# A two-layer transformer forward on one core: context transfers issued in the FFN with its norm, the output projection inside the int8 attention, casts moved between engines, root tables loaded early

## The chip, the cores and the metric

The kernel is one program for one core of a Trainium2 chip. Its engines run side by side and meet at semaphores: TensorE (PE in the profile; PEld is its weight load), VectorE (DVE), ScalarE (ACT), GpSimd (POOL), and SyncE (SP), which here only issues transfers to the core's 16 DMA engines. The metric is device time in microseconds of one execution. Lower is better.

## The reference, cut to what matters

```python
x = x + _L0_xattn_ref(_layernorm(x), ctx_2048, ...)   # fp8 self and cross attention
x = x + _L0_attn_ref(_layernorm(x), W_Q, W_K, W_V, W_O)          # causal, 16 heads
x = x + _L0_ffn_ref(_layernorm(x), gate_w, up_w, down_w)         # block-scaled fp8 FFN
x = x + _L1_xattn_ref(_layernorm(x), ctx_2048, Wq, bq, Wkv, bkv, Wp, bp)
x = x + _L1_attn_ref(_layernorm(x), wq, wk, wv, wo)              # decaying linear attention
x = x + _L1_ffn_ref(_layernorm(x), gate_w, w_gate_up, ...)       # 32 experts

# _L1_xattn_ref: 16 heads of 32, int8 rounding of q, k, v, 8 bits for the weights
q, k, v = _fq_sym(q, -1), _fq_sym(k, -1), _fq_sym(v, 2)
attn = softmax(einsum('bhqd,bhkd->bhqk', q, k)); attn = _fq_unsigned(attn, -1)
out = einsum('bhqk,bhkd->bhqd', attn, v).transpose(...).reshape(B, N, C)
return out @ Wp + bp
```

`x` is 256 tokens by 512 and the context 4096 by 512, both float32. `_layernorm` divides by the square root of the variance plus 1e-5.

## The kernel before, in words

The residual `x_res` stays in SBUF as two tiles of 128 tokens (`NT` = 2) by 512. The program is a row of stages (`Stage`). Each has its own memory and semaphores, and ends with the semaphores cleared and a barrier over all engines. So no engine starts a stage before the last one has left the stage ahead, SP included; an engine has left when its instructions are done, and for SP that means that they are issued, not that the data has landed.

`layernorm_stage` (L109) is used ahead of three stages: "ln1" ahead of the causal attention, "ln2" ahead of the FFN, "ln4" ahead of the decay attention. GpSimd writes 1e-5 to `eps`. VectorE takes mean and variance of both tiles (`s_var`). ScalarE waits for `eps` and then for each variance and takes the root (L150); a table load for the root stands right ahead of the first one, behind its wait. VectorE inverts and scales (L139, L140), TensorE transposes, and ScalarE and VectorE each copy a half of `xT`. Meanwhile SP issues the transfers that `loads` names.

- ln1's loads: the weights of head pair 0 of the causal attention (`wqkv[0]`), three units of FFN weights, `wo[0]`, and those of pair 1 (`wqkv[1]`, `wo[1]`).
- ln2's loads (`context_loads`, L1180): the context for the int8 attention in four transfers of 2 MB, and four small ones, of which the last is `vbias`, 128 rows of 4 bytes. The transposed `xT2` that ln2 makes is not read; the FFN reads `xn`.
- ln4's loads: `wkv`, `wq`, `rope`, `decay`, `wo` of group 0, then the same four of group 1.

`ffn_stage` (L1043) quantises and restores each normed tile in blocks (`mx_dequantise`, nine VectorE instructions), transposes it, and runs eight steps of gate, up and down products. Its weights are in SBUF by then. It has no work for SP or GpSimd.

`int8_cross_attention_stage` (L1236) goes over `CC` = 4 chunks of `HC` = 4 heads. `int8_order` writes one order of steps, and each engine walks it and does its part. A "slot" is 512 context positions of one tile of queries (u = 2·head + tile): a "first" product whose peak VectorE takes (L1753), and, two u later, a "second" product whose exponential ScalarE takes (L1633). Every second slot has a "turn": TensorE transposes the 8-bit weights of a head (L1510) into one of two PSUM banks `b`, ScalarE (L1640) or VectorE (L1774) casts them to `probT`, and "weigh" multiplies them with the values (L1523). A head has eight turns, j = 0 to 7. `cast_on_vector` says which engine casts: VectorE the even j, in all chunks but the last with one exception in the chunk's last head. In the last chunk there are no key and value products left to make for a next one, and in its last two heads no "first" products either. At the end of a chunk "finish" folds the sums (L1536, L1541) and VectorE writes `outT` (L1779 to L1781).

`projection_stage` (L1814, named "xout") follows as a stage of its own: it loads `w` (1 MB) and `bias`, multiplies `outT` by `w`, and adds both to the residual. Then comes ln4.

The lines that the prediction speaks of:

```python
for kc in range(KC):                                                   # L1181
    sp.dma_start(ctxT[:, kc, :], A["ctxT"][:, kc, :]).then_inc(s_ctx, 16)
...
def cast_on_vector(h, j):                                              # L1298
    return j % 2 == 0 and not (j % 4 == 2 and h % HC == HC - 1 and h // HC + 1 < CC)
...
self.nc.clear_and_free_semaphores(self.sems)                           # Stage.__exit__
self.nc.all_engine_barrier()
```

Of the kernel before, what the change touches and what calls it, by code (L numbers as in the profile page):

```python
# [108 lines left out]
def layernorm_stage(nc, name, C, x, xT, xn=None, loads=None):  # L109

    with Stage(nc, name) as st:
# [4 lines left out]
        std = st.sb("std", [P, NT])  # L116
# [3 lines left out]
        with nc.Block() as block:  # L120
# [641 lines left out]
def causal_attention_stage(nc, C, xT, A, x, ffn_weights, early, loads):  # L762
# [8 lines left out]
    with Stage(nc, "causal") as st:  # L771
# [30 lines left out]
        with nc.Block() as block:  # L802

            @block.sync
            def _(sp):
# [9 lines left out]

                for p in range(NP):
# [226 lines left out]
def ffn_stage(nc, C, xn, weights, x):  # L1043
# [3 lines left out]
    with Stage(nc, "ffn") as st:  # L1047
        deq = [st.sb(f"deq{e}", [P, DM]) for e in range(2)]
# [11 lines left out]
        names = "dequantised turned copied gate_up exp used down dve"  # L1060
        s_q, s_t, s_c, s_g, s_e, s_u, s_dn, s_dve = (st.sem(n) for n in names.split())
        steps = [(f, t) for f in range(NF) for t in range(NT)]
        with nc.Block() as block:

            @block.vector
            def _(dve):
                link = Chain(dve, s_dve).after
                for t in range(NT):
                    mx_dequantise(dve, link, xn[:, t, :], stat, power[:, :], shifted[:, :], deq[t][:, :]).then_inc(s_q, 1)
# [17 lines left out]
            def _(act):  # L1087
                for t in range(NT):
# [57 lines left out]
def build_middle(nc, C, A, x, early):  # L1146
    with ExitStack() as right:
        with ExitStack() as memory:
            weights = memory.enter_context(nc.sbuf_tensor("ffn_weights", [P, FFN_UNITS, 4, P], F32))
            with ExitStack() as inner:  # L1150
# [10 lines left out]
                def loads(sp):  # L1161
# [5 lines left out]
                    sp.dma_start(wqkv[1][:, :, :, :], A["wqkv0"][1]).then_inc(s_w[1], 16)  # L1167
                    sp.dma_start(wo[1][:, :, :], A["wo0"][1]).then_inc(s_wo[1], 16)
# [19 lines left out]
            xn = memory.enter_context(nc.sbuf_tensor("xn2", [P, NT, DM], F32))  # L1188
            xT = memory.enter_context(nc.sbuf_tensor("xT2", [P, KC, TOK], F32))
            layernorm_stage(nc, "ln2", C, x, xT, xn=xn, loads=context_loads)  # L1190
            ffn_stage(nc, C, xn, weights, x)
# [44 lines left out]
def int8_cross_attention_stage(nc, C, A, residual, ctxT, s_ctx, weights, outT):  # L1236
# [8 lines left out]
    with Stage(nc, "int8") as st:  # L1245
# [29 lines left out]
        std = st.sb("std", [P, NT])  # L1275
# [22 lines left out]
        def cast_on_vector(h, j):  # L1298
            return j % 2 == 0 and not (j % 4 == 2 and h % HC == HC - 1 and h // HC + 1 < CC)
# [12 lines left out]
        for step in order:  # L1312
# [7 lines left out]
            if what in ("turn", "key turned", "value turned", "query turned"):  # L1320
# [6 lines left out]
                 "eps var std normed x_turned xT_act xT_dve q_done q_kept q_rounded q_parts")  # L1327
        (s_a, s_aa, s_ad, s_b, s_ba, s_bd, s_vq, s_kf, s_kp, s_pk, s_sc,
         s_out, s_put, s_dve, s_hi, s_rest, s_mid, s_vm, s_vc, s_sum, s_sumc, s_fold, s_kd, s_kk,
         s_eps, s_var, s_std, s_norm, s_xt, s_xa, s_xd, s_qm, s_qk, s_qr, s_qp) = (st.sem(n) for n in names.split())  # L1330

        s_wq = st.sem("wq_loaded")
# [4 lines left out]
        with nc.Block() as block:  # L1337

            @block.sync
            def _(sp):  # L1340
# [12 lines left out]
                for c in range(1, CC):  # L1353
                    load_keys(c)
                    load_values(c)

# [27 lines left out]
            def _(pe):  # L1384
# [158 lines left out]

                pe.wait_ge(s_ctx, 16 * KC)
# [1512 lines left out]
```

## Time and profile before

| | |
|---|---|
| time, median of three runs | 2641.4 us (2641.16 to 2645.72) |
| the profiled execution: its own time, its span | 2642.37 us, 2640.6 us |
| TensorE busy, share of the span | 88% |
| VectorE busy, share of the span | 68% |
| ScalarE busy, share of the span | 47% |
| mean granted TensorE clock | 0.948 of 2.4 GHz |

The span is the time between the first and the last recorded instruction. A timeline row has the start in us from the start of the span, the duration in us, the engine, the line, the instruction, what it writes and reads, and in brackets how long the engine had been idle and what ended that. SPq is SP issuing a transfer; its duration is that of the issue. A PE row for a float32 product counts two instructions for each `matmul` of the code. A window row has the stretch, its length, the busy time of each engine, the mean granted clock as a share of full speed, the share of time that the DMA engines were busy, and GB/s.

### The profile page before, as it was taken

The numbers are of one execution on the slowest core, as the hardware profiler recorded it, in microseconds if no ns is written. First come the engines' busy times: TensorE is split into PE (matmuls) and PEld (weight loads), VectorE is DVE, ScalarE is ACT, GpSimd is POOL, SyncE is SP. The second block draws the span as 40 slices with busy tenths as digits, with TensorE's granted clock in tenths as the row PEclk, the third lists the DMA queues.
The fourth block names the chain that finished last, engine by engine and source line by source line (L and its number), as shares of the span: only waits on it lengthen the run. The fifth ranks groups of instructions, "written<-read, shape, count | busy, mean of one in ns | idle before, by whom it ended". The sixth has DMA issues, their size and how long they took to land. (4 is left out here: it accounts for less than half of the span.)

```text
span 2640.6 us, 32466 instructions
## 1 busy us (share of the span) xinstructions
PE 2326.4 (88%) x11672; PEld 1586.5 (60%) x11672; DVE 1799.9 (68%) x3545; ACT 1252.7 (47%) x2207; POOL 503.7 (19%) x411
## 2 busy tenths in 40 slices
PE   3779999999999999967994988788888779999998
PEld 2556666666666665546772455545555437777776
DVE  7855777777777779776784966777777843464444
ACT  4443466666656666533442024676666853211111
POOL 7710033333333243420000011111101000000000
PEclk9879999999999999988997999999999969899999
DMA  3231100000010000024443000000000005456662
GB/s 133 107 135 36 36 17 29 8 29 28 13 32 9 29 9 13 0 80 183 168 144 137 0 21 10 1 10 1 6 5 1 1 20 196 180 219 230 224 226 75
DMA packets 47067, 184.89 MB, mean 70 GB/s; under 512 B 6272, under 2 KB 11136, under 8 KB 36672
## 3 DMA queue, kind: packets, MB, share of 16 engines
q1 hardware_dynamic: 46912, 182.86, 19.1%
q8 instruction: 93, 1.52, 0.2%
q14 instruction: 62, 0.51, 0.1%
HBM read 173.93 MB, written 8.91 MB: 69 GB/s over the span
## 5 line engine op out<-in xcount | busy, mean ns | idle before, releaser
L402 PE MATMUL wide_a<-wide_w,ctxT 128*128 128x256 f32 (+1 forms) x2048 | 436.1, 366 | 2.8 <-POOL wide_eps L371 2.8
L402 PEld LDWEIGHTS wide_a<-wide_w,ctxT 128*128 128x128 f32 x2048 | 367.0, 190 | 76.3 <-issue 35.7
L384 POOL TENSOR_TENSOR wide_sums<-wide_sums,wide_s 128x512 f32<-128x512 f32 x224 | 302.0, 1348 | 458.2 <-ACT wide_s L532 445.0
L1633 ACT ACTIVATE int_prob<-int_a,int_shift,int_qscale 128x512 uint8<-128x512 f32 x256 | 199.1, 786 | 103.5 <-PE int_a L1499 102.9
L427 PE MATMUL wide_scores<-wide_q,wide_keysT 128*128 128x512 f32 x512 | 238.4, 604 | 10.8 <-ACT wide_s L528 10.8
L437 PE MATMUL wide_o<-wide_s,wide_values 128*128 128x512 f32 x512 | 232.5, 597 | 3.5 <-ACT wide_s L532 3.5
L528 ACT COPY wide_s<-wide_scores 128x512 f32<-128x512 f32 x256 | 148.6, 586 | 180.0 <-PE wide_scores L427 168.6
L1753 DVE TENSOR_REDUCE int_peaks<-int_a 128x1 f32<-128x512 f32 x256 | 169.6, 685 | 60.0 <-PE int_a L1499 57.8
L1499 PE MATMUL int_a<-int_keys,int_qrows 96*128 96x512 bf16 x512 | 166.0, 408 | 41.8 <-DVE int_peaks L1753 34.8
L590 DVE TENSOR_TENSOR wide_top<-wide_top,wide_s 128x512 f32<-128x512 f32 x240 | 165.7, 691 | 15.4 <-ACT wide_s L528 9.6
L427 PEld LDWEIGHTS wide_scores<-wide_q,wide_keysT 128*128 128x128 f32 x512 | 87.9, 189 | 146.9 <-ACT wide_s L528 86.0
L2231 PEld LDWEIGHTS moe_bank<-moe_xb,moe_gate_up 128*128 128x128 f32 (+1 forms) x1536 | 162.0, 183 | 8.3 <-issue 8.3
L2231 PE MATMUL moe_bank<-moe_xb,moe_gate_up 128*128 128x96 f32 (+1 forms) x1536 | 162.6, 266 | 4.3 <-issue 4.3
L566 DVE BATCH_NORM_STATS2 wide_stats<-wide_keys 128x6 f32<-128x128 f32 x256 | 61.7, 283 | 141.7 <-ACT wide_values L510 138.1
L437 PEld LDWEIGHTS wide_o<-wide_s,wide_values 128*128 128x128 f32 x512 | 96.1, 191 | 99.7 <-issue 93.4
L603 DVE TENSOR_TENSOR wide_s<-wide_s,wide_peak_rows 128x2048 f32<-128x2048 f32 x64 | 146.9, 2296 | 0.8
L1415 PE MATMUL int_vp<-int_wk,ctxT_again 128*128 128x128 f32 x1024 | 131.4, 285 | 3.0 <-PEq L77 2.2
L1415 PEld LDWEIGHTS int_vp<-int_wk,ctxT_again 128*128 128x128 f32 x1024 | 127.7, 200 | 8.3 <-issue 4.8
L508 ACT COPY wide_keys<-wide_a 128x256 f32<-128x256 f32 x128 | 46.7, 365 | 172.4 <-PE wide_a L402 172.3
L532 ACT ACTIVATE wide_s<-wide_s 128x2048 f32<-128x2048 f32 x64 | 122.4, 1912 | 5.5 <-DVE wide_s L603 4.8
L1499 PEld LDWEIGHTS int_a<-int_keys,int_qrows 96*128 96x128 bf16 x512 | 44.4, 101 | 114.5 <-DVE int_peaks L1753 59.7
L1377 POOL TENSOR_TENSOR int_rest<-int_kf,int_parts 128x512 f32<-128x512 f32 x32 | 37.0, 1157 | 387.7 <-ACT int_parts L1605 387.7
(416 smaller groups left out, 4277.1 us busy)
## 6 DMA issues: line engine op xcount, KB each, us to landing
moe_gate_up<-hbm_m_gu SPq DMA_DIRECT2D x34, 1408.0 KB, 6.2
moe_down<-hbm_m_down_a SPq DMA_DIRECT2D x34, 512.0 KB, 7.0
causal_wqkv<-hbm_wqkv SPq DMA_DIRECT2D x8, 1536.0 KB, 6.8
ctxT<-hbm_ctxT SPq DMA_DIRECT2D x4, 2048.0 KB, 14.8
oproj_raw<-hbm_wproj SPq DMA_DIRECT2D x8, 1024.0 KB, 5.3
ctxT_again<-hbm_ctxT SPq DMA_DIRECT2D x4, 2048.0 KB, 14.3
moe_down<-hbm_m_down_b SPq DMA_DIRECT2D x34, 192.0 KB, 7.3
wide_unit<-hbm_ffn_units SPq DMA_DIRECT2D x24, 256.0 KB, 2.6
```

The lines of the kernel that those rows point to most:

```text
L384: ins = pool.tensor_tensor(sums[0][:, :], before, part[:, j, :], ALU.add)
L402: mm = pe.matmul(a[h][:, j, cols], ctxT[:, kc, t * P:(t + 1) * P], w[g % 2][:, kc, cols], start=(kc == 0), stop=(kc == KC - 1))
L427: pe.matmul(sp_[j % 2][:, :], keysT[:, j, :], q[:, :], start=True, stop=True).then_inc(s_s, 1)
L437: mm = pe.matmul(o[g % 2][:, :], values[m % VR][:, j, :], s[m % SR][:, j, :], start=(c == 0 and j == 0), stop=(c == QPG - 1 and j == 3))
L528: act.copy(s[n % SR][:, j, :], sp_[j % 2][:, :]).then_inc(s_se, 1)
L590: link(dve.tensor_tensor(top[:, :], before, s[n % SR][:, j, :], ALU.max))
L603: dve.tensor_tensor(s[m % SR][:, :, :], s[m % SR][:, :, :], peak_rows[:, :].unsqueeze(1).to_broadcast([P, 4, COLS]), ALU.subtract).then_in ...
L1415: mm = pe.matmul(vp[:, t * P:(t + 1) * P], ctxT[:, kc, i * P:(i + 1) * P], wk[:, kc, :], start=(kc == 0), stop=(kc == KC - 1))
L1499: pe.matmul(a[n % 4][:, :], qrows[0:3 * HD, h, t * P:(t + 1) * P], keys[0:3 * HD, h % HC, j * 512:(j + 1) * 512], start=True, stop=True).t ...
L1633: act.activation(prob[u % 4][:, j * 512:(j + 1) * 512], a[n % 4][:, :], ACT.Exp, bias=shift[:, u % NU:u % NU + 1], scale=qscale[:, t, h:h ...
L1753: dve.tensor_reduce(peaks[u % 2][:, j:j + 1], a[n % 4][:, :], AX.X, ALU.max).then_inc(s_ad, 1)
L2231: mm = pe.matmul(dst[0:m, j, :], wgu[i][:, kc, z * EI + f0:z * EI + f0 + m], xb[q % 2][:, kc, e % BATCH, :], start=(kc == 0), stop=(kc == ...
```

## The change

Five edits:

1. The stage ln2 is gone. `ffn_stage` norms `x` itself, and its SP issues `context_loads`. The transposes and copies to `xT2` are gone.
2. The transfers of `wqkv[1]` and `wo[1]` move from ln1 to the head of the causal stage's SP queue; those of group 1 from ln4 to the head of the decay stage's.
3. The stage xout is gone. The int8 stage loads its weights once the last chunk's values have been turned (into the tile `vq`, and the bias into `kf[0]`), VectorE adds the bias ahead of the last "finish", and TensorE multiplies after it in PSUM banks `a`, chunks 0 to 2 ahead of the wait for the last part of `outT`.
4. In the last chunk VectorE casts six of a head's eight turns, all but j = 3 and 7, where it cast the four even ones.
5. In ln1, ln4, the FFN and the int8 stage ScalarE takes a root of `eps` as soon as `eps` is written, ahead of the wait for the variance. The result is not used.

```diff
@@ layernorm_stage, the same in the int8 stage's roots()
                 act.wait_ge(s_eps, 1)
+                act.activation(std[:, NT:], eps[:, 0:1], ACT.Sqrt)
                 for t in range(NT):
                     act.wait_ge(s_var, t + 1)
@@ causal_attention_stage, SP
+                sp.dma_start(wqkv[1][:, :, :, :], A["wqkv0"][1]).then_inc(s_w[1], 16)
+                sp.dma_start(wo[1][:, :, :], A["wo0"][1]).then_inc(s_wo[1], 16)
                 for p in range(NP):
@@ ffn_stage
+            @block.sync
+            def _(sp):
+                loads(sp)
+
+            @block.gpsimd
+            def _(pool):
+                pool.memset(eps[:, :], EPS).then_inc(s_eps, 1)
...
                 for t in range(NT):
+                    link(dve.bn_stats(stats[:, t, :], x[:, t, :]))
+                    dve.bn_aggr(mv[:, t, :], stats[:, t, :]).then_inc(s_var, 1)
+                for t in range(NT):
+                    dve.wait_ge(s_std, t + 1)
+                    link(dve.reciprocal(rstd[:, t:t + 1], std[:, t:t + 1]))
+                    link(dve.tensor_scalar(xn[:, t, :], x[:, t, :], mv[:, t, 0:1], rstd[:, t:t + 1], ALU.subtract, ALU.mult))
                     mx_dequantise(dve, link, xn[:, t, :], stat, power[:, :], shifted[:, :], deq[t][:, :]).then_inc(s_q, 1)
@@ build_middle
-            layernorm_stage(nc, "ln2", C, x, xT, xn=xn, loads=context_loads)
-            ffn_stage(nc, C, xn, weights, x)
+            ffn_stage(nc, C, x, weights, context_loads)
@@ int8_cross_attention_stage
         def cast_on_vector(h, j):
-            return j % 2 == 0 and not (j % 4 == 2 and h % HC == HC - 1 and h // HC + 1 < CC)
+            if h // HC + 1 == CC:
+                return j % 4 != 3
+            return j % 2 == 0 and not (j % 4 == 2 and h % HC == HC - 1)
...
+                sp.wait_ge(s_b, use_b["value turned", CC - 1, 3] + 1)
+                sp.wait_ge(s_kp, CC * NS)
+                sp.dma_start(wp, A["x_wp"]).then_inc(s_wp, 16)
+                sp.dma_start(bp[:, :], A["x_bp"]).then_inc(s_wp, 16)
...
+                def project_out():
+                    pe.wait_ge(s_wp, 32)
+                    for who, sem in (("act", s_aa), ("dve", s_ad)):
+                        pe.wait_ge(sem, counts["a " + who])
+                    for c in range(CC):
+                        if c == CC - 1:
+                            pe.wait_ge(s_put, CC)
+                        for t in range(NT):
+                            mm = pe.matmul(a[t][:, :], outT[:, c, t * P:(t + 1) * P], wp[:, c, :], start=(c == 0), stop=(c == CC - 1))
...
                     elif what == "finish":
+                        if x == CC - 1:
+                            dve.wait_ge(s_wp, 32)
+                            for t in range(NT):
+                                link(dve.tensor_tensor(residual[:, t, :], residual[:, t, :], bp[:, :], ALU.add))
                         finish(x)
...
+                    dve.wait_ge(s_xo, t + 1)
+                    dve.tensor_tensor(residual[:, t, :], residual[:, t, :], a[t][:, :], ALU.add)
@@ build_int8_attention
-        projection_stage(nc, "xout", outT, 4, A["x_wp"], A["x_bp"], x)
@@ decay_attention_stage, SP (the same four go from ln4's loads)
+                sp.dma_start(wkv[1][:, :, :], A["d_wkv"][1]).then_inc(s_w[1], 16)
+                sp.dma_start(wq[1][:, :, :], A["d_wq"][1]).then_inc(s_w[1], 16)
+                sp.dma_start(decay[1][:, :, :, :], A["decay"][1]).then_inc(s_wo[1], 16)
+                sp.dma_start(wo[1][:, :, :], A["d_wo"][1]).then_inc(s_wo[1], 16)
```

## Rows read from the trace of the kernel before

**Rows 1.** Timeline from ln2 to the head of the FFN

```profile
1404.69 0.10 POOL L129 MEMSET ln_eps<- 128x1 f32 x1 [182.29 <-POOLq L77]
...
1405.51 0.18 DVE L136 BATCH_NORM_AGGREGATE ln_mv<-ln_stats 128x2 f32<-128x6 f32 x1
...
1406.06 1.28 ACT L150 ACT_TABLE_LOAD   x1 [7.29 <-DVE ln_mv L136]
...
1407.88 0.55 DVE L140 TENSOR_SCALAR xn<-x_res,ln_mv,ln_rstd 128x512 f32<-128x512 f32 x1
...
1411.21 12.97 SPq L1186 DMA_DIRECT2D int_vbias<-hbm_x_bv  x1
1425.06 0.69 DVE L746 TENSOR_REDUCE ffn_stat<-xn 128x16 f32<-128x512 f32 x1 [13.88 <-PEq L77]
```

**Rows 2.** Timeline of the int8 attention's end and the stage xout

```profile
2158.30 0.42 DVE L1762 COPY int_part_out<-int_sums 128x256 f32<-128x256 f32 x1 [1.17 <-PE int_sums L1523]
...
2158.89 1.10 PE L1541 MATMUL int_vp<-int_part_out,int_fold 128*32 128x256 f32 x8
...
2160.95 0.35 DVE L1781 TENSOR_SCALAR outT<-outT,int_value_scale 128x256 f32<-128x256 f32 x1
...
2167.77 9.64 PE L1833 MATMUL xout_acc<-xout_w,outT 128*128 128x512 f32 x16 [7.79 <-DMA xout_bias<-hbm_x_bp]
...
2177.53 0.69 DVE L1843 TENSOR_TENSOR x_res<-x_res,xout_acc 128x512 f32<-128x512 f32 x1 [2.02 <-PE xout_acc L1833]
```

**Rows 3.** Windows: last chunk (three stretches), its last head, the projection

```profile
2098.90:2113.00 14.10, 11.06 (x84) 4.71 (x82) 13.87 (x22) 14.10 (x33) 0.00 (x0) 1.00 0.01 2
2114.40:2133.20 18.80, 15.36 (x99) 6.35 (x98) 16.55 (x31) 16.47 (x37) 0.00 (x0) 0.82 0.00 1
2133.20:2149.00 15.80, 11.17 (x75) 4.36 (x73) 5.74 (x8) 15.80 (x36) 0.00 (x0) 0.67 0.00 0
2149.50:2158.00 8.50, 7.01 (x68) 3.73 (x65) 5.23 (x5) 4.05 (x4) 0.00 (x0) 0.50 0.01 2
2167.70:2172.90 5.20, 5.13 (x6) 2.19 (x7) 0.69 (x1) 0.00 (x0) 0.00 (x0) 0.51 0.00 0
```

**Rows 4.** Windows: end of ln2, the FFN's first step, its rest

```profile
1412.00:1425.00 13.00, 0.00 (x0) 0.00 (x0) 0.00 (x0) 0.00 (x0) 0.00 (x0) 0.50 1.01 432
1431.90:1441.00 9.10, 9.09 (x19) 4.11 (x20) 2.93 (x5) 0.00 (x0) 0.00 (x0) 0.80 0.01 2
1441.00:1536.40 95.40, 85.07 (x211) 37.67 (x209) 79.04 (x104) 11.34 (x18) 0.00 (x0) 0.95 0.00 0
```

**Rows 5.** Timeline: first product of the causal stage and the transfer ahead of it

```profile
1214.42 0.33 SPq L1162 DMA_DIRECT2D causal_wqkv<-hbm_wqkv  x1
...
1221.30 6.29 PEld L864 LDWEIGHTS causal_proj<-xT,causal_wqkv 128*128 128x128 f32 x16 [1.83 <-DMA causal_wqkv<-hbm_wqkv]
```

**Rows 6.** DMA issues: line, count, KB, us to landing of that transfer

```profile
causal_wqkv<-hbm_wqkv SPq DMA_DIRECT2D x1, 1536.0 KB, 6.5
```

**Rows 7.** Timeline: first product of the decay stage

```profile
2185.98 0.50 PEld L1905 LDWEIGHTS decay_pq<-xT,decay_wkv 128*128 128x128 f32 x2 [1.84 <-DMA decay_wq<-hbm_d_wq]
```

**Rows 8.** Timeline: first query product of the int8 stage

```profile
1545.55 0.30 PEld L1454 LDWEIGHTS int_a<-int_vq,int_prob 128*128 128x128 f32 x2 [2.09 <-DMA int_probT<-hbm_x_bq]
```

**Rows 9.** Timeline of VectorE in the last chunk

```profile
2100.07 2.48 DVE L1753 TENSOR_REDUCE int_peaks<-int_a 128x1 f32<-128x512 f32 x4
2102.47 1.22 DVE L1774 CAST int_probT<-int_b 128x1024 bf16<-128x1024 uint8 x1
2103.60 1.28 DVE L1753 TENSOR_REDUCE int_peaks<-int_a 128x1 f32<-128x512 f32 x2
```

**Rows 10.** Timeline of ScalarE in the last chunk

```profile
2104.60 1.07 ACT L1640 CAST int_probT<-int_b 128x1024 bf16<-128x1024 uint8 x1
2105.49 0.86 ACT L1633 ACTIVATE int_prob<-int_a,int_shift,int_qscale 128x512 uint8<-128x512 f32 x1
```

**Rows 11.** DMA queue, kind: packets, MB, share of 16 engines; 1403 to 1440

```profile
q14 instruction: 3, 0.02, 0.2%
```

More of the change, by code:

```diff
@@ L1040, in _, with ffn_stage @@
                     dve.tensor_tensor(x[:, t, :], x[:, t, :], acc[t][:, :], ALU.add)
-def ffn_stage(nc, C, xn, weights, x):
+def ffn_stage(nc, C, x, weights, loads):
     NF = 4
     with Stage(nc, "ffn") as st:
+        xn = st.sb("xn", [P, NT, DM])
+        stats = st.sb("stats", [P, NT, 6])
+        mv = st.sb("mv", [P, NT, 2])
+        eps = st.sb("eps", [P, 1])
+        std = st.sb("std", [P, NT + 1])
+        rstd = st.sb("rstd", [P, NT])
         deq = [st.sb(f"deq{e}", [P, DM]) for e in range(2)]
@@ L1059, in ffn_stage @@
         acc = [st.ps(f"acc{t}", [P, DM]) for t in range(NT)]
-        names = "dequantised turned copied gate_up exp used down dve"
-        s_q, s_t, s_c, s_g, s_e, s_u, s_dn, s_dve = (st.sem(n) for n in names.split())
+        names = "eps var std dequantised turned copied gate_up exp used down dve"
+        s_eps, s_var, s_std, s_q, s_t, s_c, s_g, s_e, s_u, s_dn, s_dve = (st.sem(n) for n in names.split())
         steps = [(f, t) for f in range(NF) for t in range(NT)]
         with nc.Block() as block:
+            @block.sync
[4 more added lines that the diff above has]
+                pool.memset(eps[:, :], EPS).then_inc(s_eps, 1)
             @block.vector
@@ L1087, in _ @@
             def _(act):
+                act.wait_ge(s_eps, 1)
+                act.activation(std[:, NT:], eps[:, 0:1], ACT.Sqrt)
+                for t in range(NT):
+                    act.wait_ge(s_var, t + 1)
+                    act.activation(std[:, t:t + 1], mv[:, t, 1:2], ACT.Sqrt, bias=eps[:, 0:1]).then_inc(s_std, 1)
                 for t in range(NT):
@@ L1568, in _ @@
                         finish(x)
+                project_out()
             @block.scalar
@@ L1573, in roots @@
                     act.wait_ge(s_eps, 1)
+                    act.activation(std[:, NT:], eps[:, 0:1], ACT.Sqrt)
                     for t in range(NT):
@@ L1810, in _ @@
                     elif what == "finish":
+                        if x == CC - 1:
+                            dve.wait_ge(s_wp, 32)
+                            for t in range(NT):
+                                link(dve.tensor_tensor(residual[:, t, :], residual[:, t, :], bp[:, :], ALU.add))
                         finish(x)
[L1814 to L1843 removed]
+                for t in range(NT):
+                    dve.wait_ge(s_xo, t + 1)
+                    dve.tensor_tensor(residual[:, t, :], residual[:, t, :], a[t][:, :], ALU.add)
 def build_int8_attention(nc, C, A, x, context):
```

55 lines of the change are left out of this document (14 added, 41 removed).

## The prediction

> **What bounds the kernel now.** I read the timeline first, from the end of each stage to the first work of the next, since four of the five edits lie there. The largest gap is ahead of the FFN [rows 1]. VectorE finds its first work there at 1425.06 after 13.88 us of idling, put down to TensorE's sequencer, which is how a barrier shows. The engine that held the barrier is SP: its issue of `vbias`, a transfer of 0.5 KB, lasted 12.97 us, from 1411.21 to 1424.18. It stands behind 8 MB of context, and the window row shows what it waited for: the DMA engines busy all the time at 432 GB/s, and no other engine with any work [rows 4]. So 13 us of the kernel are an issue that waits for room behind a transfer that nobody needs before the int8 stage, more than 100 us later [rows 8].
>
> The second place is the stage xout [rows 2]. The products that fold the sums end at 2158.89 + 1.10 = 2159.99, and `outT` is whole at 2160.95 + 0.35 = 2161.30. TensorE's next product starts at 2167.77, after 7.79 us of idling that ended with the bias's landing. The products take 9.64 us, and the last add ends at 2178.22.
>
> The third is the int8 stage's last chunk [rows 3]. The reader should see in the first row that ScalarE is busy for 14.10 of 14.10 us and VectorE for 13.87: both are full. In the third row ScalarE is still full, and VectorE works 5.74 of 15.80 us. In the rows from the second on TensorE's granted clock sinks to 0.82, 0.67 and 0.50.
>
> **Edits 1 and 5 in the FFN.** Without ln2, the FFN's statistics start where ln2's did. The first restoring instruction follows the norm of tile 0 directly: 1407.88 + 0.55 = 1408.43 in place of 1425.06, which is 16.6 us. It no longer waits for the transposes, the copies to `xT2`, a barrier or SP. The early root adds to that. The table load started at 1406.06, which is 0.37 after the variance (1405.51 + 0.18 = 1405.69). Tied to `eps`, written at 1404.79, with the same 0.37 it starts at 1405.16, so 0.90 earlier. The extra root has a price: from the load's end at 1407.34 to the norm at 1407.88 there are 0.54 us, in which one root, its handing over and the reciprocal lie; one root more costs less than that, and I take 0.25. Gain 0.65 (0.36 to 0.90). Tile 1's norm is 0.7 us longer in VectorE's queue, but it is covered by TensorE's first step of 9.1 us [rows 4]. TensorE starts that step at half clock before and, having idled since the causal stage, will again. Sum: 17.3 us, bounds 16.5 and 17.9 with the clock's rise taken as uncertain by half a microsecond. The stream of context goes on under the FFN, which touches no transfer. If the FFN's work were not there to cover it, it would cost the 13 us again. Nothing queues behind `vbias` in the new SP queue, and the next one to want SP is the int8 stage.
>
> **Edits 2 and 5 around the other norms.** The first product of the causal stage starts at 1221.30 and waited for `wqkv[0]` [rows 5], issued at 1214.42 and landed 6.5 us later [rows 6], at 1220.92. The early root brings `xT` forward by up to 0.65 us, but only 1221.30 − 1220.92 = 0.38 of it can be used. I take 0.3 (0 to 0.4). `wqkv[1]` and `wo[1]` keep their place in the order of the one SP queue; unit 3's transfer stood behind them before too, and now stands behind two more issues in the same stage. Nothing for that. The decay stage's first product waited for a transfer too [rows 7], and so did the int8 stage's first query product [rows 8]. So the root's 0.65 us is hidden there: 0 each, bound 0.65 for both together.
>
> **Edit 3.** Twelve of the sixteen instructions of the projection need no part of the last chunk, and can start at 2159.99 in place of 2167.77: 7.8 us. The other four wait for `outT`, which is whole 1.3 us later, when at most three of the twelve are done. So what is late next is TensorE itself. Its duration hangs on the clock. Six instructions took 5.13 us at 0.51 [rows 3], 0.86 each, and the other ten the remaining 4.5 us of 9.64, 0.45 each. All at half clock would take 13.7 us, all at full clock 7.2. The clock ahead of it is 0.50 although TensorE is busy for 7.01 of 8.50 us [rows 3], so it will start at half as before, and I keep 9.64.
>
> The Trainium skill ("TensorE: Matmul & The Clock Gate", Part 4: PE-mode transpose) says that transposes don't count as busy for the clock in the way that matmuls do. That agrees with the 0.50 beside 7.01 of 8.50 us, much of which is transposes; by this rule the products keep their 9.64 us, and if transposes counted like all other work they would take 7.2.
>
> Against it stands VectorE's end of the last head. It was busy 5.23 of 8.50 us [rows 3]. Two more casts and two bias adds come in ahead of the copy at 2158.30. A cast takes 2103.60 − 2102.47 = 1.13 us of its time [rows 9], an add 0.69 [rows 2]: 5.23 + 2.26 + 1.38 = 8.87. That is 0.4 over the stretch without a single wait for a bank; three casts in a row on one engine, with two banks, wait at times. I take 1.2 us (0.4 to 2.0).
>
> **Edit 4.** Per head two casts leave ScalarE, where each takes 2105.49 − 2104.60 = 0.89 [rows 10], and cost VectorE 1.13 each [rows 9]. Head 12: VectorE has 13.87 + 2.26 = 16.13 us of work in a stretch of 14.10, so 2.0 more, of which I let the change of heads take 0.3: cost 1.7 (1.0 to 2.3). Head 13: 16.55 + 2.26 = 18.81 in 18.80, so it just fits if no wait is left. The waits came from TensorE at a clock of 0.82 and stay in part; 1.4 (0 to 2.3). Head 14: ScalarE is the full one and loses 1.78 us; TensorE at half clock then limits, so 0.9 gained (0 to 1.8). Net cost 2.2 us, bounds a gain of 0.8 and a cost of 4.6.
>
> **Sum.** 17.3 + 0.3 + 7.8 − 1.2 − 2.2 = 22.0 us. The profiled execution took 2642.37 us for a span of 2640.6; less 22.0 it is 2620.4. It lay 1.0 us above the median of the runs, so 2619.4 is the forecast of the median.
>
> **Rivals.**
>
> *The casts pay.* ScalarE sets the pace of the whole last chunk: it has no idle time in two of three rows [rows 3], and reductions of peaks back to back cost VectorE only (2102.47 − 2100.07)/4 = 0.60 each [rows 9]. If VectorE's queue gives way, the cost of 2.2 becomes a gain of 1.8: 26.0 us, 2615.4. Against it stands VectorE's 13.87 of 14.10.
>
> *The clock stays low to the end.* With VectorE as the limit TensorE has less to do, and its clock, 0.82 to 0.50 already, is half through the last chunk and the whole projection: 13.7 us in place of 9.64, and 2.3 us more in the chunk. 22.0 − 4.1 − 2.3 = 15.6 us, 2625.8. Against it: float32 products raised it after 5.2 us in xout.
>
> *The stream holds the FFN.* The engines' own instructions come by DMA too: queue 14 shows three packets between 1403 and 1440 [rows 11], with the engines at 432 GB/s beside them. If an engine's next block of code waits until the context has landed, the FFN starts as late as before, and edit 1 has moved nothing: 22.0 − 17.3 = 4.7 us, 2636.7. The causal stage speaks against it: it began under transfers, and its first product waited for its weights alone [rows 5]. The Trainium skill ("Runtime: NRT & Kernel Launch", Instruction fetch mechanics) says that each sequencer fetches its code in blocks over a DMA queue of its own while it runs; by that a block is late only if its DMA takes longer than the block ahead of it lasts, and the trace shows no such wait.
>
> *Slower: the FFN at half clock.* TensorE works 85.07 of 95.40 us there at 0.95 [rows 4]. If the clock, after the cold start beside the transfers, stayed at half for all of it, that work would be 85.07 · (0.95/0.50 − 1) = 77 us longer: 2696. From about 25 us at half clock on it would eat the gain. Against it: in its first step it rose to a mean of 0.80 within 9.1 us.
>
> **How the numbers follow.** Forecast 0.66, casts that pay 0.14, clock low to the end 0.12, stream holds the FFN 0.05, FFN at half clock 0.03. The range takes in the second and the third: 2614 to 2626. Beyond it lie some of the first two rivals and the last two, together less than 0.2. 0.2% is 5.3 us, about what a measurement of this kernel can tell from no change. The first three cases are faster by more, the fourth lies just within, the last is slower: 0.92, 0.05, 0.03.
>
> **What would show it.** Right: no issue of SP ends a wait in the FFN; its first restoring instruction comes about 3 us after the stage's start, where 20 lay between; the causal stage's first product is 0.3 us earlier; VectorE's idle time in heads 12 and 13 is gone and head 12's stretch is near 16 us; the projection's first product follows the fold at once and its last ends some 10 us later. Wrong: an idle TensorE or VectorE in the FFN while the context lands, a clock of 0.5 past the FFN's first step or through the whole projection, or heads 12 and 13 as long as before.

## The result, and the profile after

The kernel after takes 2612.26 us (median of 4 runs, 2606.3 to 2616.58), the kernel before, run beside it, 2641.9 (4 runs, 2641.16 to 2645.72). The ratio is 0.9883, with a 95% interval of 0.9861 to 0.9906. That is 29.6 us faster. The forecast was 2619.4 with a range of 2614 to 2626: the sign is right, and the time lies 1.7 us below the range.

The profiled execution took 2606.3 us for a span of 2604.5, at a mean granted clock of 0.959 where 0.948 stood before. It was the fastest of the four, so the two profiles differ by 36.1 us in span, and not all of that is the change's. I read the timeline again from the end of each stage to the first work of the next. First the FFN, which answers to [rows 1]:

```profile
1398.77 2.13 SPq L1208 DMA_DIRECT2D ctxT_again<-hbm_ctxT  x4
...
1398.77 1.28 ACT L1112 ACT_TABLE_LOAD   x1 [5.92 <-DVEq L77]
...
1399.60 0.18 DVE L1087 BATCH_NORM_AGGREGATE ffn_mv<-ffn_stats 128x2 f32<-128x6 f32 x1
...
1400.07 0.20 ACT L1112 ACTIVATE ffn_std<-ffn_eps 128x1 f32<-128x1 f32 x1
...
1400.69 0.55 DVE L1091 TENSOR_SCALAR ffn_xn<-x_res,ffn_mv,ffn_rstd 128x512 f32<-128x512 f32 x1
...
1401.27 0.69 DVE L747 TENSOR_REDUCE ffn_stat<-ffn_xn 128x16 f32<-128x512 f32 x1
...
1405.14 13.70 SPq L1212 DMA_DIRECT2D int_vbias<-hbm_x_bv  x1
...
1408.12 0.29 PEld L1150 LDWEIGHTS ffn_gate<-ffn_weights,ffn_xT 128*128 128x128 f32 x1 [1.07 <-ACT ffn_xT L1118]
```

The first restoring instruction comes 2.50 us after the stage's start (1401.27 − 1398.77). The issue of `vbias` still takes 13.70 us, from 1405.14 to 1418.84, but the first gate product starts at 1408.12 in the middle of it: nobody waits for SP now. The window rows that answer to [rows 4] show the context's stream (DMA share about 1) under the FFN's first step, and the rest of the stage at the clock of before:

```profile
1408.10:1417.00 8.90, 8.88 (x16) 3.88 (x17) 3.66 (x7) 0.00 (x0) 0.00 (x0) 0.75 1.02 433
1417.00:1507.30 90.30, 80.73 (x205) 36.06 (x203) 79.01 (x104) 10.66 (x17) 0.00 (x0) 0.96 0.06 20
```

Second, the projection in the int8 block, which answers to [rows 2]. The fold ends at 2131.26 + 1.22 = 2132.48 and TensorE goes straight on; `outT` is whole at 2133.78 and nothing waits for it:

```profile
2131.26 1.22 PE L1572 MATMUL int_vp<-int_part_out,int_fold 128*32 128x256 f32 x8
2132.41 0.50 PEld L1583 LDWEIGHTS int_a<-int_vq,outT 128*128 128x128 f32 x2 [0.81 <-issue]
2132.41 8.96 PE L1583 MATMUL int_a<-int_vq,outT 128*128 128x512 f32 x16
...
2133.43 0.35 DVE L1826 TENSOR_SCALAR outT<-outT,int_value_scale 128x256 f32<-128x256 f32 x1
...
2141.41 0.69 DVE L1863 TENSOR_TENSOR x_res<-x_res,int_a 128x512 f32<-128x512 f32 x1 [0.17 <-PE int_a L1583]
```

Third, the last chunk, answering to [rows 3]. The windows are cut at the start of ScalarE's first exponential of heads 13, 14 and 15, at the end of its last, and at the fold's end; the fifth is the projection. A head's weights are cast while the next one's exponentials are made, so the first four are named by the head that is cast, 12, 13, 14 and the last:

```profile
2067.00:2088.30 21.30, 16.19 (x130) 7.52 (x129) 18.27 (x31) 18.59 (x39) 0.00 (x0) 0.98 0.18 63
2088.30:2106.80 18.50, 14.01 (x97) 5.20 (x96) 18.23 (x33) 14.96 (x35) 0.00 (x0) 0.96 0.01 1
2106.80:2119.90 13.10, 12.42 (x75) 5.73 (x73) 7.68 (x9) 13.10 (x34) 0.00 (x0) 0.53 0.00 0
2119.90:2132.50 12.60, 9.12 (x93) 4.85 (x93) 9.52 (x13) 2.98 (x4) 0.00 (x0) 0.60 0.00 1
2132.40:2141.40 9.00, 8.97 (x17) 3.68 (x16) 1.89 (x4) 0.00 (x0) 0.00 (x0) 0.79 0.00 0
```

VectorE fills head 13 (18.23 of 18.50) and ScalarE head 14 (13.10 of 13.10). By the same cuts the kernel before took 20.57, 18.81, 14.92, 11.88 and 9.64.

Last, the first products of the causal, the int8 and the decay stage, which answer to [rows 5], [rows 8] and [rows 7]:

```profile
1215.49 0.50 PEld L867 LDWEIGHTS causal_proj<-xT,causal_wqkv 128*128 128x128 f32 x2 [2.47 <-DMA causal_wqkv<-hbm_wqkv]
...
1520.95 0.30 PEld L1485 LDWEIGHTS int_a<-int_vq,int_prob 128*128 128x128 f32 x2 [0.74 <-DMA int_probT<-hbm_x_bq]
...
2149.03 0.50 PEld L1928 LDWEIGHTS decay_pq<-xT,decay_wkv 128*128 128x128 f32 x2 [2.25 <-DMA decay_wq<-hbm_d_wq]
```

**Where the 36.1 us are.** I cut both profiles at marks (the first or last instruction of a group) and subtract. Every experiment below is cut in the same way.

| stretch | before | after | gained | predicted |
|---|---|---|---|---|
| start to the first `wide_a` product | 197.46 | 192.32 | 5.1 | 0 |
| from there to ln1 | 1017.02 | 1016.65 | 0.4 | 0 |
| ln1 to the first causal product | 6.85 | 6.52 | 0.3 | 0.3 |
| causal stage, to its last add | 182.58 | 182.49 | 0.1 | 0 |
| last add to the first gate product | 28.01 | 10.13 | 17.9 | 17.3, with the next row |
| gate product to the int8 stage | 106.95 | 107.51 | −0.6 | |
| int8 stage to its first query product | 6.69 | 5.33 | 1.4 | 0 |
| from there to the first exponential of head 13 | 548.26 | 546.02 | 2.2 | 0 |
| casting heads 12, 13, 14 | 54.30 | 52.89 | 1.4 | −2.2 |
| last head, to the fold's end | 11.88 | 12.61 | −0.7 | −1.2 |
| fold to the projection | 7.79 | −0.07 | 7.9 | 7.8 |
| projection | 9.64 | 8.96 | 0.7 | 0 |
| ln4 to the first decay product | 6.85 | 5.98 | 0.9 | 0 |
| rest | 456.31 | 457.15 | −0.8 | 0 |

The large terms stand as predicted. About 7 us of the 36.1 lie in stretches that the change does not touch (start, wide stage, causal stage, the way to head 13, rest), and the small terms came out about 7 us better than forecast. Unchanged stretches vary from one profile to the next. Over the fourteen profiles here the one from the first `wide_a` product to ln1 took 1016.7 to 1020.4 us and the causal stage 180.4 to 185.7; the way from gate product to int8 stage took 106.9 to 107.8 in the three kernels (before, edit 3 alone, edit 4 alone) that share its code and all ahead of it. So a term under 1 us there is not told from chance by one pair of profiles.

### The profile page after: what moved, and what is told of

It reads as the page before. It is cut to its first block and busy times, and to the rows that moved or that the text cites. A ratio compares the mean times of both kernels' runs of the same rounds, so it can differ in the third digit from the quotient of the medians.

```text
span 2604.5 us, 32400 instructions
## 1 busy us (share of the span) xinstructions
PE 2315.5 (89%) x11664; PEld 1578.5 (61%) x11664; DVE 1805.1 (69%) x3552; ACT 1244.9 (48%) x2202; POOL 502.8 (19%) x411
```

## The experiments

**Edit 1 alone.** The kernel before with the FFN's own norm and the context transfers in its SP queue, without the early root.

```diff
-            layernorm_stage(nc, "ln2", C, x, xT, xn=xn, loads=context_loads)
-            ffn_stage(nc, C, xn, weights, x)
+            ffn_stage(nc, C, x, weights, context_loads)
```

> The kernel before with edit 1 alone (the norm inside the FFN, the context transfers issued there, no early root). My theory: the FFN's first gate product is reached 17.0 to 17.3 us sooner than in the kernel before, measured from the end of the causal stage, and nothing else changes, so the median falls by 17 us. Rival (the code or the transfers of one stage disturb others, or the stream gives something back): the FFN's first product is 17 us sooner but the median moves by another amount, 22 us or more if the earlier stages gain 5 us as they did in the profile of the kernel after, under 14 us if the int8 stage gives some back.

Measured: 2621.66 us beside 2641.16 of the kernel before, ratio 0.9931 (0.9916 to 0.9946), which is 19.5 us and by the interval 14 to 22. The last add stands 11.41 us ahead of the first gate product where it was 28.01: 16.6 gained, 0.4 short of what was expected. The FFN behind it took 108.23 where it took 106.95, so 15.3 are left at the int8 stage. The profile has the short start (192.34) and, from the first peak product to head 12's first exponential, the 448.0 us of the kernel after again, where 450.1 stood before.

**Edit 3 alone, edit 4 alone, and the kernel after without edit 4.**

```diff
-            return j % 2 == 0 and not (j % 4 == 2 and h % HC == HC - 1 and h // HC + 1 < CC)
+            if h // HC + 1 == CC:
+                return j % 4 != 3
+            return j % 2 == 0 and not (j % 4 == 2 and h % HC == HC - 1)
```

For edit 3 alone the casts' rule stays and the int8 block gets the projection:

```diff
+                project_out()
...
-        projection_stage(nc, "xout", outT, 4, A["x_wp"], A["x_bp"], x)
```

> The kernel before with edit 3 alone (the projection and its adds inside the int8 block, casts shared out as before). My theory: the last residual add ends 8.5 us sooner after the end of the last chunk's fold, which is what the kernel after showed, and the two bias adds cost VectorE nothing that anybody waits for; 8 us in the median. The prediction's term was 7.8 less a small part of 1.2, so 7 us. Rival (the fewer casts of ScalarE made the last head short enough to hide the adds): without edit 4 the stretch of the last head is 1 us or more longer than in the kernel before and the edit alone brings under 7 us.

Measured: 2633.9 us, ratio 0.997 (0.996 to 0.998), 7.3 us faster by the medians. In the profile the projection follows the fold at once (7.9 gained) and takes 8.45 us, so the last add comes 9.1 us sooner after the fold. The last head takes 11.93 where it took 11.88 with no add in it, so the two bias adds cost nothing that anybody waits for. The rival falls.

> The kernel before with edit 4 alone (six of eight casts on VectorE in the last chunk's heads). By the prediction's sum: 2.2 us slower, head 12 by 1.7, head 13 by 1.4, head 14 faster by 0.9. By what the kernel after showed: head 12 0.8 slower, head 13 0.3 faster, head 14 1.8 faster, the last chunk's end 0.7 or more faster, so the median unchanged or up to 1.5 us lower. By the rival that the casts pay: 1.8 us faster.

Measured: 2642.02 us, ratio 1.0006 (0.9997 to 1.0015). Head 12 took 0.6 longer, head 13 1.6 longer, head 14 1.8 less, the last head 0.9 longer: a loss of 1.4 us. For heads 12 to 14 alone, which the prediction's cost of 2.2 is about, it is 0.4; the last head's 0.9 belongs to its 1.2. The projection behind it took 0.7 less, 8.97 us, though here it is still a stage of its own.

> The kernel after with edit 4 undone. If edit 4 is worth 1.3 us or so beside the other edits (my theory now): 1 to 2 us slower than the kernel after, by the time from the first exponential of head 12 to the end of the fold. By the prediction's sum it would be 2.2 us faster. Whether the first stage is again 5 us shorter than in the kernel before tells whether that gain belongs to the kernel after or to chance: by chance it may be anything from 0 to 6 us here.

Measured: 2611.53 us, 0.7 below the kernel after's 2612.26, less than the spread of either. In the profile heads 12 to 15 and the projection together took 75.05 us, in the kernel after 74.46. Its first stages took 197.93 us where the kernel after had 192.32, with the same code: chance. The rows are the windows over the self-attention ahead of the `wide_a` products, of before, of after and of this one:

```profile
133.10:197.40 64.30, 49.85 (x192) 37.89 (x192) 36.37 (x96) 29.13 (x84) 10.33 (x23) 0.80 0.32 135
```

```profile
132.10:192.30 60.20, 46.01 (x192) 34.91 (x193) 36.28 (x96) 29.04 (x84) 10.36 (x23) 0.86 0.34 145
```

```profile
133.70:197.90 64.20, 49.21 (x192) 37.55 (x193) 36.31 (x96) 29.10 (x84) 10.29 (x23) 0.81 0.32 136
```

The same work, 192 instructions, takes 60.2 us at a clock of 0.86 and 64.2 at 0.81.

**What in edit 1 brings what.** Two kernels made from the one before. The first keeps ln2 and only issues the context transfers in the FFN. The second only turns the order in ln2's loads around:

```diff
 def context_loads(sp):
+    (the four small transfers, unchanged)
     for kc in range(KC):
         sp.dma_start(ctxT[:, kc, :], A["ctxT"][:, kc, :]).then_inc(s_ctx, 16)
-    (the four small transfers)
```

> The kernel before, with the context transfers issued at the FFN's start but ln2 kept as a stage of its own. Edit 1's 16.6 us from the causal stage's last add to the FFN's first gate product (28.0 in the kernel before, 11.4 with edit 1 alone) have two parts. If the 13 us stall is one and the stage boundary with its second transposition the other, this kernel reaches that product after 15.0 us, gains 13.0, and the merged norm is worth 3.6. Rival (SP's stall simply moves to a place where something waits for it): 28 us, or an idle TensorE inside the FFN or at the int8 stage's start. Second question: with edit 1 the stretch from the int8 stage's first peak product to head 12 was 448.0 us in three kernels, without it 450.1 in three. If the work around it sets that, it stays 450.1 or 448.0; if it is only where the low stretches of the clock fall, any value from 446 to 452 may come.

Measured: 2630.95 us, ratio 0.9955 (0.9941 to 0.9969). The first gate product comes 15.09 us after the last add: 12.9 gained, so the stall is 12.9 of the 16.6 and the merged norm 3.7. The `vbias` issue takes 14.01 us here, beside a working FFN:

```profile
1411.74 1.90 SPq L1186 DMA_DIRECT2D ctxT_again<-hbm_ctxT  x4
1411.80 0.69 DVE L746 TENSOR_REDUCE ffn_stat<-xn 128x16 f32<-128x512 f32 x1 [0.96 <-PEq L77]
...
1418.09 14.01 SPq L1190 DMA_DIRECT2D int_vbias<-hbm_x_bv  x1
```

So the stall moved to a place where nothing waits for it. From the int8 stage's first peak product to head 12 it took 451.4 us, a third level beside 450.1 and 448.0.

> The kernel before with the order of the transfers in ln2 changed: the four small ones (key and value weights, their biases) first, the four of the context behind them. If the last issue waits for room behind the 8 MB of context, nothing small stands behind it now and only a part of the context's own issues may wait: the FFN's first gate product comes 15.0 to 18 us after the causal stage's last add in place of 28.0, a gain of 10 to 13. Rival (any eighth transfer waits until earlier ones have ended): still 28 us, or about 25.

Measured: 2630.65 us, ratio 0.9945 (0.9925 to 0.9964), and 14.87 us to the gate product. The rows are all of SP's issues:

```profile
1402.61 0.65 SPq L1181 DMA_DIRECT2D int_wk<-hbm_x_wkv  x1
1403.31 0.62 SPq L1182 DMA_DIRECT2D int_kbias<-hbm_x_bk  x1
1404.29 0.55 SPq L1183 DMA_DIRECT2D int_wv<-hbm_x_wkv  x1
1404.89 0.61 SPq L1184 DMA_DIRECT2D int_vbias<-hbm_x_bv  x1
1405.55 2.15 SPq L1186 DMA_DIRECT2D ctxT_again<-hbm_ctxT  x4
```

The same eight issues, and none stalls: `vbias` takes 0.61 us, the four of the context 2.15 together. A change of order alone brings 13.1 of edit 1's 16.6 us. The rival, a limit on the number of transfers under way, this run does not settle by itself: when its eighth issue came, at 1407.14, the first two transfers had landed, while in the kernel before none of the seven ahead of `vbias` had. The trace of the kernel before does settle it. By their landing times seven transfers were under way at the first of these issues and nine at the second, and both went through:

```profile
2184.18 0.45 SPq L2476 DMA_DIRECT2D decay_wo<-hbm_d_wo  x1
```

```profile
2287.23 0.49 SPq L2152 DMA_DIRECT2D moe_down<-hbm_m_down_a  x1
```

So the number alone does not stall an issue (the next one, with ten under way, took 1.53). Nor does every small transfer stall behind the 8 MB: in the kernel before the issues of the first two (256 and 64 KB) took 0.66 and 0.68 us, the third (256 KB) 3.00 and the fourth (0.5 KB) 12.97. What fills up between them is open.

**The early root, and edit 2.** The kernel after without the four extra roots, and the kernel after with the second group of weights issued in ln1 and ln4 again.

```diff
-                act.activation(std[:, NT:], eps[:, 0:1], ACT.Sqrt)
```

> The kernel after without the four early roots (edit 5 undone). By the profiles so far the root brings 1.3 us in the FFN (first gate product 11.4 us after the last add in place of 10.1). At the other norms three gains stand beside it: 0.4 at the causal stage, 1.4 at the int8 stage's first query product and 0.9 at the decay stage's first product. If the root made them all, this kernel is 3.5 to 4 us slower than the kernel after; if the decay stage's comes from edit 2 and the int8 stage's from when a transfer landed, it is 1.3 to 1.7 slower. The prediction's terms for the root were 0.65, 0.3, 0 and 0.

Measured: 2613.89 us (2609.08 to 2618.13), ratio 0.9884 (0.9862 to 0.9906), too wide to tell 1.6 from 4. The profile tells more: the four stretches are back at 11.41, 6.85, 6.79 and 6.85 us. For the FFN, the causal and the decay stage that is the root's work. For the int8 stage it is not. There the normed tiles go to TensorE, which first makes 32 key products. The rows are those products in the kernel before, in the kernel after and in this one, each 0.15 us behind its stage's start:

```profile
1539.01 3.81 PE L1415 MATMUL int_vp<-int_wk,ctxT_again 128*128 128x128 f32 x32 [2.21 <-PEq L77]
```

```profile
1515.78 3.81 PE L1446 MATMUL int_vp<-int_wk,ctxT_again 128*128 128x128 f32 x32 [2.24 <-PEq L77]
```

```profile
1525.83 5.44 PE L1444 MATMUL int_vp<-int_wk,ctxT_again 128*128 128x128 f32 x32 [2.24 <-PEq L77]
```

All times from the stage's start: the root brings the first normed tile from 3.37 to 2.43, but TensorE starts to transpose it at 3.69 with the root and without (kernels before and after), and the copies of both end at 5.56. So the root gained nothing there. What ended last in the kernel after was still the transfer of `bq`, landed at 5.30 where it was 6.65 before. Without the roots it landed at 5.49, but TensorE made the key products at a granted clock of 0.66 in place of 1.00, started to transpose at 5.32, and the query product came at 6.79. All seven profiles with the root have the full clock there, and of the seven without it three; whether the root has a part in that is not shown.

At the decay stage the root did the work. The rows are the timeline's first issue and first product of the new stage, and the landing of the `decay_wq` that was issued at 2154.83, by the view of that tensor:

```profile
2161.31 0.33 SPq L1899 DMA_DIRECT2D decay_wkv<-hbm_d_wkv  x1
2161.33 0.50 PEld L1925 LDWEIGHTS decay_pq<-xT,decay_wkv 128*128 128x128 f32 x2 [1.84 <-DMA decay_wq<-hbm_d_wq]
```

```profile
DMA to landing us min/median/max: 5.8/5.8/5.8
```

The row puts the wait down to the transfer. But the transfer landed at 2154.83 + 5.8 = 2160.6, and the product started with the other engines' first instructions of the stage, at 2161.3, as soon as the barrier let them through. What ended last was the norm, its last copy and the barrier.

For edit 2 undone (the comments are not the kernel's):

```diff
-                sp.dma_start(wqkv[1][:, :, :, :], A["wqkv0"][1]).then_inc(s_w[1], 16)   # causal stage, and so in the decay stage
+                    sp.dma_start(wqkv[1][:, :, :, :], A["wqkv0"][1]).then_inc(s_w[1], 16)   # ln1, and so in ln4
```

> The kernel after with edit 2 undone: the second group of weights is issued ahead of the stage again, in ln1 and ln4. If the shorter queue made the decay stage's first product 0.9 us earlier, it goes back to 6.85 us after the stage's start from 5.95, and the kernel is 0.9 us slower. If the early root made it, it stays at 5.95 and the time is that of the kernel after, which was the prediction's term of 0 for edit 2.

Measured: 2609.14 us (2605.72 to 2609.52), ratio 0.9872 (0.9853 to 0.9892). The decay stage's first product comes after 6.07 us, the causal stage's after 6.26, where the profiles with edit 2 and the root have 5.94 to 6.27 and 6.32 to 6.52. The time is 3 us below the kernel after's first measurement, so it was run again beside it.

**Four kernels side by side.** The kernel after; edit 4 undone; six of eight casts on VectorE in heads 13 and 14 alone; edit 2 undone.

```diff
-                return j % 4 != 3
+                return j % 4 != 3 if h % HC in (1, 2) else j % 2 == 0
```

> The kernel after, unchanged, beside three variants of it on one chip. The fixed stretches should repeat within 0.1 us: 10.1 from the causal stage's last add to the FFN's first gate product, 448.0 from the int8 stage's first peak product to head 12's first exponential, 13.1 for head 14. The first stages, to the first product of the wide matmuls, have been anything from 192.2 to 197.7 us in ten profiles, kernels before and after alike, so the profile's total may differ from the first one's by up to 5 us; the median should be 2610 to 2613.

> The kernel after with edit 4 undone, again, now beside the kernel after. Profiles so far: with the new casts head 12 takes 0.6 us longer, head 13 0.5 less (in one of five 1.6 longer), head 14 1.8 less, head 15 0.8 longer and the projection behind it 0.6 longer. Net 0.3 gained. My theory: this kernel is 0 to 1 us slower than the kernel after. The prediction's term (a cost of 2.2 plus most of 1.2) would make it 2 to 3 us faster.

> The kernel after, with six of eight casts on VectorE in heads 13 and 14 alone; heads 12 and 15 share them four and four as before. If each head's balance is its own, head 12's stretch is back at 20.7 us (21.3 in the kernel after), head 15's at 11.9 (12.6), heads 13 and 14 stay at 18.5 and 13.1, and the projection at 8.4 to 9.0: 1.3 us or more faster than the kernel after. If a head hands its backlog to the next, head 13 or 14 takes it back and the total is the same.

> The kernel after with edit 2 undone, again, beside the kernel after. In its profile the causal stage's first product was 0.2 us sooner, the decay stage's 0.1 later, so edit 2 is worth nothing and this kernel has the time of the kernel after within 1 us; its median was 2609.1 in the other call, and if edit 2 truly costs something it is 2 us or more faster here as well.

Measured, beside 2642.88 us of the kernel before: after 2612.17 (ratio 0.9882, 0.9865 to 0.9898); edit 4 undone 2611.44 (0.9878, 0.9862 to 0.9895); heads 13 and 14 alone 2607.35 (0.9864, 0.9848 to 0.9881); edit 2 undone 2611.46 (0.9879, 0.9862 to 0.9895). By stretches, with the kernels from above:

| | head 12 | 13 | 14 | last | projection | sum |
|---|---|---|---|---|---|---|
| before | 20.57 | 18.81 | 14.92 | 11.88 | 9.64 | 75.8 |
| edit 3 alone | 20.58 | 18.82 | 14.91 | 11.93 | 8.45 | 74.7 |
| edit 4 alone | 21.18 | 20.46 | 13.09 | 12.81 | 8.97 | 76.5 |
| after | 21.32 | 18.48 | 13.09 | 12.61 | 8.96 | 74.5 |
| after, again | 21.29 | 18.16 | 13.09 | 12.93 | 8.94 | 74.4 |
| edit 4 undone, again | 20.72 | 19.21 | 14.92 | 11.93 | 8.31 | 75.1 |
| six in heads 13, 14 alone | 20.79 | 18.99 | 13.09 | 11.93 | 7.80 | 72.6 |

The windows of head 13 in edit 4 alone, in the kernel after again, and in the last kernel, one fence each (cut 0.1 to 0.3 us ahead of the marks):

```profile
2113.60:2134.10 20.50, 17.88 (x98) 6.95 (x97) 18.89 (x35) 15.27 (x34) 0.00 (x0) 0.67 0.00 1
```

```profile
2098.80:2116.90 18.10, 13.61 (x97) 5.14 (x96) 17.86 (x31) 14.95 (x34) 0.00 (x0) 1.00 0.01 1
```

```profile
2098.30:2117.30 19.00, 17.14 (x98) 7.01 (x97) 18.14 (x31) 15.12 (x34) 0.00 (x0) 0.71 0.01 1
```

Head 12 costs 0.6 with six casts, head 14 gives 1.8 whatever the clock, and the last head costs 0.7 to 1.0 with the projection behind it 0.6 more; in the last kernel heads 12, 14 and the last head are each at the value that their own casts give elsewhere. Head 13 moves with TensorE's clock: 18.2 us at 1.00 and 20.5 at 0.67 with the same casts, against 18.8 to 19.2 with four. But it took 19.0 at 0.71, and 1.5 us is much for the step from 0.71 to 0.67. The kernel with 20.5 has six casts in head 12 as well, that with 19.0 four, and VectorE has more to do in its window (18.89 us against 18.14). So work handed on from head 12 is not excluded where the clock is low. The last kernel was expected to keep head 13's 18.5 and took 19.0; its projection, expected at 8.4 to 9.0, took 7.80. Six casts in heads 13 and 14 alone give 1.8 us over the kernel after in their profiles, 1.1 of it in the projection; the intervals of the two times overlap, so the 4.8 us between the medians are not established. Edit 4 undone is 0.7 us slower in the profile and 0.7 faster by the medians: no difference that these runs can tell. Its profile took 451.6 us to head 12, with the code of the kernel after up to there. So the levels of 448.0, 450.1 and 451.4 are not edit 1's either.

Edit 2 is worth nothing that these runs can tell: 2611.46 and 2612.17 side by side.

## Why the prediction was right and wrong

**The FFN, 17.3: right.** From the last add to the int8 stage it took 134.96 us before and 117.64 after: 17.3. Inside the term two errors cancel. The early root gives 1.28 us, not 0.65 (11.41 against 10.13). I had its table load wait for `eps`; it starts with the stage, at 1398.77 with the memset's own start, and the extra root costs 0.13 (load's end 1400.05 to 1400.18, the first variance's root), not 0.25. The other way, the FFN takes 0.6 longer from its first product on, 1.3 with edit 1 alone; the 0.6 lies within the spread of unchanged code. The mechanism is the one that was predicted, the agreement to a tenth is luck.

**Edit 3, 7.8: right in its mechanism and 0.7 to 1.2 us small.** The gap is gone (7.79 to −0.07). "I keep 9.64" was the term that was mis-sized: the products took 8.94 to 8.96 in five profiles of this order of casts, and 8.3 to 8.45 with the old casts. They start at half clock as said, but it rises inside them sooner than in the kernel before:

```profile
2132.40:2137.00 4.60, 4.60 (x8) 2.05 (x8) 1.20 (x3) 0.00 (x0) 0.00 (x0) 0.60 0.00 0
2137.00:2141.30 4.30, 4.30 (x11) 1.63 (x9) 0.69 (x1) 0.00 (x0) 0.00 (x0) 1.00 0.00 0
```

The first 4.6 us have a mean of 0.60 and the next 4.3 run at full clock, where xout had 0.51 over its first 5.2 us [rows 3]. The Trainium skill's rule on transposes and the clock ("TensorE: Matmul & The Clock Gate", Part 4: PE-mode transpose) gave 9.64 against 7.2 for the case that they count; the times lie between. The start at half clock, behind a last head in which TensorE was busy for 9.12 of 12.60 us, agrees with the rule, but no run varies the transposes. With the new casts the place made no difference (8.97 us as a stage of its own, with edit 4 alone), with the old ones it made 1.2 (9.64 and 8.45), so what sets the moment of the rise is open.

**The last head, −1.2: the size right, the reason half.** It cost 0.7 to 1.0, all from the two casts. The bias adds cost nothing (11.93 against 11.88): with the casts too VectorE is busy for 9.52 of 12.60 us.

**Edit 4, −2.2: this step failed, in two ways.** For head 14 the prediction said that "TensorE at half clock then limits, so 0.9 gained". ScalarE limited, and its two casts came off in full: 14.92 to 13.09 in every profile, also at 0.53. For head 12 it added 2.26 us to VectorE's 13.87 of 14.10 and took 1.7 of it as cost; VectorE was that much busier, but 0.6 to 0.7 came through to ScalarE's next head. The window of 14.10 us had left out the end of the head, where VectorE was idle from 2113.00 to 2114.40, and the new work fell into that. The rows are the head behind its first 5.1 us, of before and of after:

```profile
2098.90:2114.40 15.50, 11.82 (x91) 5.12 (x90) 13.87 (x22) 14.71 (x34) 0.00 (x0) 1.00 0.01 2
```

```profile
2072.10:2088.30 16.20, 12.78 (x94) 4.93 (x92) 15.89 (x24) 13.74 (x32) 0.00 (x0) 1.00 0.19 76
```

That is the sign that was named, idle time gone and about 16 us, at a third of the cost. For head 13 its 1.4 came out once, at a clock of 0.67 (edit 4 alone: 1.6); at 0.71 it was 0.2, and at a high clock, as in the kernel after, a gain of 0.3 to 0.7. The sum was −2.2 − 1.2; the profiles of the kernel after have +1.4 − 0.7. That is 4.1 us of the miss, and the rival "the casts pay" was the nearer one.

**The roots at the int8 and the decay stage, 0 each: this failed too, for a reason of its own.** "So the root's 0.65 us is hidden there: 0 each" kept the landing of the transfers where it was in the one trace of before. In the kernel before `decay_wq` landed at 2179.50 + 6.4 = 2185.9 and the barrier let the product start at 2185.98: the two ended together, so the named releaser was not the whole cause, and with that landing the root would have been worth about 0.1, by my estimate from these rows. But the landing moves. In the seven profiles with the root it came 5.6 to 5.9 us after the issue, and the product 5.94 to 6.27 us after the stage's start. In the seven without the root it came 5.8 to 6.8 us after the issue, and the product at 6.84 to 7.15, also where the landing was early. At the int8 stage the root is hidden as predicted, behind TensorE's key products. The 1.4 us there are `bq`'s earlier landing, as the list of issues of before and of after has it (KB, us to landing):

```profile
int_probT<-hbm_x_bq SPq DMA_DIRECT2D x1, 256.0 KB, 6.3
```

```profile
int_probT<-hbm_x_bq SPq DMA_DIRECT2D x1, 256.0 KB, 5.0
```

It came with every kernel that has no ln2, and pays only where TensorE has the full clock at the stage's start. Together the two stages gave 2.2 us in the profile, beside a bound of 0.65.

**The rest is unchanged code.** The way from the query product to head 13's first exponential took 548.26 us before and 546.02 after. Over all fourteen profiles it has three levels 1.1 to 2.1 us apart, and the start up to the first `wide_a` product lies anywhere from 192.3 to 197.9 us. By terms the change is worth 17.3 + 0.3 + 2.2 + 7.9 + 0.7 + 0.7 = 29.1 us, where the last 0.7 is edit 4 with the last head; the medians say 29.6 and 30.7. Against the forecast's 22.0 that is 7.1 more: 4.1 from the casts and the last head, 2.2 from the two transfers, 0.7 from the projection. The range took in a gain of the casts or a low clock, one at a time, and these three terms all moved one way.

**The rivals.** The stream did not hold the FFN (it began under a DMA share of about 1), the FFN's clock was 0.96 past its first step, and the clock rose inside the projection: these three fell. Of the casts that pay, given 0.14, about half came true.

## What to carry to other kernels

A tiny transfer issued behind megabytes can hold its queue's engine, and through a barrier every engine: put it first, or put the issue where no barrier follows. A row that names a transfer as what ended a wait has not shown that the compute chain was much earlier; add up the chain too, and let the landing vary (here by 1.2 to 1.7 us from kernel to kernel), before a gain is called hidden. The reverse holds as well: a stretch that goes back when an edit is undone is not yet that edit's; look at what ended last in both. Where the clock changes what a shift of work costs, cost it as a pair of cases and not as one sum, and take first the piece that gains in both (here head 14).

## What the runs showed of the hardware

The issue stall depends on what lies ahead in the queue and not on the number of issues: 12.97 to 14.14 us for the 0.5 KB of `vbias` behind 8 MB and three smaller transfers in thirteen profiles, 2.8 to 3.3 us for the one ahead of it, 0.61 us with the small ones first. The four 2 MB issues took 1.9 to 2.2 us together in either order. Nine transfers under way did not stall an issue of the experts' stage (0.49 us at 2287.23).

The table load of an `ACTIVATE` with one wait ran ahead of that wait, at the stage's start (1398.77), while without the early root it came 0.36 us after the variance (1399.67 + 0.18 = 1399.85), as in edit 1 alone:

```profile
1400.21 1.28 ACT L1111 ACT_TABLE_LOAD   x1 [7.29 <-DVE ffn_mv L1084]
1401.51 0.48 ACT L1111 ACTIVATE ffn_std<-ffn_mv,ffn_eps 128x1 f32<-128x1 f32 x2
```

The root starts 0.02 us behind the load. The Trainium skill ("ScalarE: Activation LUTs", What ACT_TABLE_LOAD costs) gives about 1.28 us for the load and 1.38 more for a drain, 2.66 in all. The load agrees, no drain shows here in any of these stages, and what the early root hid in the FFN is 1.28 (11.41 to 10.13).

`bq` landed 6.2 to 6.6 us after its issue in all five profiles of kernels with ln2 as a stage, and 4.9 to 5.3 in all nine without it. I have no experiment on why. In the kernel before one packet of queue 8, instructions, runs among its last packets, but one does in the kernel after as well, so that is not shown to be the cause. What sets the levels of the stretch from the first peak product to head 12 is open in the same way.
